# A decoder layer in fp32 on one core: the first step's weight rounding moved to pair 5, LayerNorm roots behind the second maxima, a new order of the fourth batch, identity products between the first maxima

## What is computed

```python
def reference(x, ctx_512, ...):
    x = _layernorm(x + _L0_attn_ref(x, wq, wk, wv, wo))       # 16 heads, causal, rope
    x = _layernorm(x + _L0_xattn_ref(x, ctx, Wq, Wkv_expand, Wout))
    x = _layernorm(x + _L0_ffn_ref(x, weight1, weight2, weight3))

def _L0_ffn_ref(x, weight1, weight2, weight3):
    w1, w2, w3 = nf4_roundtrip(weight1), nf4_roundtrip(weight2), nf4_roundtrip(weight3)
    h = silu(einsum('bsd,fd->bsf', x, w1)) * einsum('bsd,fd->bsf', x, w2)
    return einsum('bsf,df->bsd', h, w3)

def _layernorm(x, eps=1e-05):
    return (x - mean(x)) / sqrt(var(x) + eps)
```

## Time and profile before

| | |
|---|---|
| median of 3 runs | 1119.15 us (1118.89 to 1129.97) |
| profiled execution | 1125.64 us, span 1123.9 us |
| mean granted clock of TensorE | 0.976 |
| PE busy | 1038.3 us (92%) |
| DVE busy | 755.5 us (67%) |
| ACT busy | 482.4 us (43%) |
| POOL busy | 439.8 us (39%) |
| chain that ended last | PE 67%, DVE 19%, issue 5%, DMA 3%, POOL 3% |

### The profile page before, as it was taken

How to read it: one execution, slowest core, us unless ns; L and a number is a source line. 1 busy time by engine, 2 the same in 40 slices (tenths; PEclk the granted TensorE clock), 3 DMA queues, 4 the chain that set the end, 5 groups by cost and what they waited for, 6 DMA issues and landing times.

```text
span 1123.9 us, 17522 instructions
## 1 busy us (share of the span) xinstructions
PE 1038.3 (92%) x6280; PEld 670.4 (60%) x6280; DVE 755.5 (67%) x1560; ACT 482.4 (43%) x587; POOL 439.8 (39%) x462
## 2 busy tenths in 40 slices
PE   9899999999999898998989998998989999999995
PEld 7545455555455454565546556555636888888884
DVE  7778658666866688559676876877673546464535
ACT  3343445554464464546654664676442212112110
POOL 3448675975786564123352432334257000000000
PEclk9899999999999999999989999999989999999998
DMA  6731586386636674646755485757445202011021
GB/s 232 216 91 30 140 220 180 90 242 179 191 84 169 189 203 102 160 92 147 208 140 125 116 202 127 166 147 183 111 135 163 83 1 105 8 38 38 1 75 38
DMA packets 92618, 145.16 MB, mean 129 GB/s; under 512 B 22507, under 2 KB 39795, under 8 KB 92275
## 3 DMA queue, kind: packets, MB, share of 16 engines
q1 hardware_dynamic: 83218, 116.49, 39.8%
q0 software_dynamic: 8000, 26.75, 8.3%
q10 hardware_dynamic: 1312, 0.79, 0.2%
HBM read 78.09 MB, written 23.73 MB: 91 GB/s over the span
## 4 chain that ended last, share of the span: by engine, by line
PE 67%; DVE 19%; issue 5%; DMA 3%; POOL 3%; ACT 2%; SPq 1%; ACTq 0%; DVEq 0%; POOLq 0%
PE att_pv L1041 11%; PE att_scores L978 7%; PE att_scores L1294 7%; PE att_pv L1294 7%; PE att_scores_T L1324 7%; PE att_scores_T L962 6%; PE att_scores_T L1014 5%; PE att_scores_T L964 5%; PE att_scores_T L963 5%; DVE att_mx L1653 4%; PE att_scores_T L1159 2%; DVE att_scores L1648 2%; DVE att_nf_zone L1808 2%; DMA att_nf_home<-nf_reciprocals 2%; DVE att_stats L1684 1%
## 5 line engine op out<-in xcount | busy, mean ns | idle before, releaser
L1461 ACT ACTIVATE att_probs<-att_scores_T 128x1024 f32<-128x1024 f32 (+2 forms) x256 | 218.3, 885 | 161.7 <-PE att_scores_T L1014 159.1
L1041 PE MATMUL att_pv<-att_probs,att_v 128*32 128x512 f32 (+3 forms) x1024 | 216.6, 539 | 7.9 <-POOL att_probs L842 7.1
L1041 PE MATMUL att_pv<-att_probs,att_ones 128*32 128x512 f32 (+3 forms) x1024 | 216.6, 539 | 0.0
L1653 DVE TENSOR_REDUCE att_mx<-att_scores 128x2 f32<-128x1024 f32 x124 | 151.5, 1222 | 86.1 <-PE att_scores L978 85.3
L978 PE MATMUL att_scores<-att_k_stack,att_q_stack 96*128 96x256 f32 (+1 forms) x504 | 168.8, 407 | 32.2 <-DVE att_mx L1653 23.1
L1648 DVE CUSTOM_DVE_ANT_0 att_scores<-att_scores,att_cmask 128x128 f32<-128x128 f32 (+3 forms) x256 | 120.9, 511 | 40.6 <-PE att_scores L978 39.4
L1014 PE MATMUL att_scores_T<-att_q_stack,att_k_stack 97*128 97x512 f32 (+2 forms) x512 | 140.3, 386 | 7.7 <-ACT att_raw L1399 2.3
L978 PEld LDWEIGHTS att_scores<-att_k_stack,att_q_stack 96*128 96x128 f32 x504 | 88.3, 195 | 80.5 <-DVE att_mx L1653 32.8
L842 POOL TENSOR_SCALAR_AFFINE_SELECT att_probs<-att_probs 128x256 f32<-128x256 f32 x128 | 59.0, 461 | 164.8 <-ACT att_probs L1461 159.5
L1014 PEld LDWEIGHTS att_scores_T<-att_q_stack,att_k_stack 97*128 97x128 f32 x512 | 87.7, 195 | 49.4 <-issue 18.9
L1547 ACT ACTIVATE att_probs<-att_scores 128x512 f32<-128x512 f32 x44 | 26.3, 598 | 208.0 <-PE att_scores L1294 208.0
(11 more groups left out here) (262 smaller groups left out, 2102.3 us busy)
## 6 DMA issues: line engine op xcount, KB each, us to landing
att_q_stack<-att_q_hi SPq DMA_DIRECT2D x128, 128.0 KB, 3.2
att_probs<-nf_x SPq DMA_DIRECT2D x28, 352.0 KB, 3.5
att_nf_home<-nf_reciprocals POOLq DMA_DIRECT2D x48, 176.0 KB, 4.8
att_q_stack<-att_q_lo SPq DMA_DIRECT2D x64, 128.0 KB, 3.6
att_k_stack<-att_k_hi SPq DMA_DIRECT2D x64, 128.0 KB, 3.5
att_nf_home<-nf_x SPq DMA_DIRECT2D x20, 352.0 KB, 3.6
w_nf<-att_nf_zone SPq DMA_DIRECT2D x192, 22.0 KB, 2.5
att_k_stack<-att_k_hi SPq DMA_DIRECT2D x64, 64.0 KB, 4.1
```

Source lines behind the costliest of these rows:

```text
L1041: last = T.matmul(pv[HD * j:HD * j + HD, sums, q0:S], lhs, pr[:, at:at + S - q0], start=(t == 0), stop=(t == TT - 1))
L1461: A.activation(probs_of(b, r)[:, 1024 * h:1024 * h + w], bank[:, 0:w], ACT.Exp, scale=SCALE).then_inc(st_free, 1)
L1653: V.tensor_reduce(mx[:, p % 2, :].rearrange("p (r t) -> p r t", r=2)[:, :, t], sco[:, :, :], AX.X, ALU.max).then_inc(sc_free, 1)
```

## The change

Five edits, which leave every result the same.

1. At the start PE multiplies the identity by itself five times ahead of each of the maxima of pair 1, t = 1, 2, 3.
2. `round_steps` leaves out pair 0 of every self attention batch, and takes pair 5 instead of leaving it out. So (1, 5) and (2, 5) carry a round each, (2, 0) and (3, 0) none. The number of rounds in self attention stays 20.
3. In batches 1 and 2 the whole of `spread` stands behind the second maxima (t = 1) of pair 2; its first part stood at the end of pair 1, its second ahead of these maxima. `scale_rows` stands behind the rounding's last pass.
4. In batch 3 the third maxima (t = 2) come directly behind the second on DVE, and the fourth ahead of pass 3, as in cross attention; on PE the projections of the next batch stand between them accordingly.
5. In batch 3 `spread` stands in one piece behind the third maxima of pair 3, and `scale_rows` of pair 4 behind the third maxima and behind pass 3.

```diff
@@ -104,7 +104,7 @@
-            if b < B and p == 5 or b == B - 1 and p > 4 or (b, p) in ((1, 0), (B, 0)):
+            if b < B and p == 0 or b == B - 1 and p > 4 or (b, p) == (B, 0):
@@ -1199,6 +1199,9 @@
             for t in range(1, TT):
+
+                for i in range(5):
+                    T.matmul(bank_for(("exp", 0, 0, 0))[:, 0:P], ident[:, :], ident[:, :], start=True, stop=True)
                 maxima(0, 1, t)
@@ -1236,7 +1239,7 @@
-                    elif crossed(b) and whats:
+                    elif late(b) and whats:
@@ -1867,8 +1870,6 @@
                         moments(b - 1, 1)
-                        if not late(b):
-                            begin_spread(range(TT))
@@ -1879,11 +1880,7 @@
-                    if b > 0 and not late(b) and p == 2:
-                        end_spread(range(TT))
-                    if b == B - 1 and p == 3:
-                        begin_spread(range(TT))
-                    if (b, p) == (B - 1, 4) or (b, p) == (NB - 1, 5):
+                    if (b, p) == (NB - 1, 5):
                         scale_rows(range(0, 2), TT - 1)
@@ -1891,22 +1888,18 @@
                     if b > 0 and not late(b) and p == 2:
-                        scale_rows(range(TT), TT - 1)
+                        spread(range(TT))
-                    quick = crossed(b) and bool(made(b + 1, p))
+                    quick = late(b) and bool(made(b + 1, p))
                     if quick:
                         maxima(*fore, 2)
-                    if crossed(b) and p == 3:
-                        begin_spread(range(TT))
                     if late(b) and p == 3:
-                        end_spread(range(TT))
+                        spread(range(TT))
-                    if b == B - 1 and p == 4:
-                        scale_rows(range(2, TT), TT - 1)
-                    if quick and b > B and p == 5:
+                    if quick and (b > B and p == 5 or (b, p) == (B - 1, 4)):
                         scale_rows(range(0, 2), TT - 1)
@@ -1928,8 +1921,10 @@
                     exceeds(end, (1, 2, 3) if beside else (3,))
-                    if quick and b > B and p == 5:
+                    if quick and (b > B and p == 5 or (b, p) == (B - 1, 4)):
                         scale_rows(range(2, TT), TT - 1)
+                    if b > 0 and not late(b) and p == 2:
+                        scale_rows(range(TT), TT - 1)
```

## The result

| | before | changed |
|---|---|---|
| median | 1120.52 us (4 runs, 1118.89 to 1129.97) | 1141.98 us (4 runs, 1138.08 to 1145.53) |
| profiled execution | 1125.64 us, span 1123.9 | 1141.23 us, span 1139.5 |
| mean granted clock | 0.976 | 0.977 |
| PE busy | 1038.3 us | 1040.1 us |

The ratio is 1.0152 (95% interval 1.0112 to 1.0192): slower by 1.5%, 17 us. The forecast was +7.7 us, 1126.8 us with a range to 1133.0. The direction was right, the size was less than half of the measured one.

A forecast was written before the change was run, and what follows sets the result against it. TensorE, busy 92% of the span, was taken to bound the kernel, so shifts of each touched step's last matmul were added: +7.7 us in sum, median 1126.8 us from 1119.15, own range 1123 to 1131, wider range 1116.0 to 1133.0.

The forecast's parts named there:

- Identity products: Start, ahead of step (0,0): products may keep the clock up, but VectorE's row bounds this stretch; -0.5 us, bounds +1.1 and -2.3.
- Rounding taken from pair 0: Steps (2,0) and (3,0): the wait for pass 3 and the rounding's length go; -1.9 and -2.1 us.
- Rounding put at pair 5: Steps (1,5) and (2,5): VectorE's passes wait for GpSimd's operations; +4.3 us each, and +1.3 each for low clock.
- A wait at (1, 7): Step (1,7): TensorE's 0.59 us wait for the rounding before goes, as its load comes sooner; -0.6 us.
- Roots behind the second maxima: Step (1,2): VectorE pays the roots after idling, +0.7 us; step (2,2): TensorE's wait and low clock go, -1.1 us.
- The fourth batch: Steps (3,2) to (3,6): waits for fourth maxima go, but pass 3 comes late; +2.0 us, bounds +0.9 and +3.4.
- pair 5 is cheap: Rival: passes slip between GpSimd's operations, both +4.3 become +0.9 and the clock stays; -1.7 us, median 1117.5; chance 0.22.
- All that is new also waits: Rival: roots in (2,2) gain nothing, fourth batch costs its upper bound, one pair 5 costs 6; 11.9 us, 1131.1; chance 0.15.
- the start: Rival: clock stays full at the start, later stretch goes, freed transfers at (3,0) pay; +3.5 us, 1122.7; chance 0.10.

## Why the prediction fell short

The terms of the forecast against the step lengths of the changed kernel's profile:

*Identity products, -0.5:* measured +0.2, and no difference in time in the run with them alone. Right in its reason, and in the price: ten records took 1.04 us (34.95 to 35.99), where 1.1 was forecast.

*Rounding taken from pair 0, -1.9 and -2.1:* -1.0 over (2, 0) and (2, 1), and -5.4 over (3, 0) and (3, 1). The direct gain is 2.3 and 2.9 us here and 1.7 to 2.6 in the other runs with the edit, near the 2.1 and 2.2 worked out. In (3, 1) the 2.5 us are the low clock that lay at 389.8 in the execution before; the runs with the products alone and with the order alone lose it too (-2.3 and -3.0), with the rounding of (3, 0) in place. Not an effect of the change, so that this pair of steps did better than forecast is luck.

*Rounding put at pair 5, +4.3 each and +1.3 for the clock:* the mechanism was right, pass by pass: three DVE passes, each 0.38 us behind a GpSimd operation. Two sizes were off. The wait in (1, 5) was 4.97, not 3.6, for GpSimd's operations stood 1.4 us earlier in the step, so that the first pass met the next one, which ends 1.1 us later in the step than the one it was to meet; the forecast took the order of before as fixed in time. Wait and rounding together, 5.7 us, stayed under the +6 named as the upper bound. In (2, 5) the wait was 3.88, close to the forecast, although the operations do not stand "in the same places" there: before, L779 begins 1.6 us into (2, 5) and 4.1 us into (1, 5). They come every 2.5 us, so in both steps one of them ends 6.5 us into the step, and this is what counts. And the low clock lasted 6.8 us in both places: (1, 5) and (1, 6) grew by 7.6 us, of which wait and rounding are 5.0 + 0.7, and (2, 5) and (2, 6) by 6.9, of which they are 3.9 + 0.7; the rest, 1.9 and 2.3 us where 1.3 was taken, is put down to the clock. The upper bound of 1.7 was too low, since a stretch can be twice as long as the one it was read from; the earlier trace rows itself has one of 10.3 us. Together 15.2 us over (1, 5), (1, 6), (2, 5) to (2, 7), against 11.2.

*A wait at (1, 7), -0.6:* measured -0.6, by luck: the runs with the products alone and with the row scaling in pair 3, in which no rounding moved, have the same.

*Roots behind the second maxima, +0.7 and -1.1:* measured +1.5 and -0.7. The signs came out as forecast, the second of them with help from the clock (1.9 us of (2, 2), see the run with the roots alone). The place was wrong: the steps themselves became shorter, and the next ones longer, by the scaling of the rounding that now comes behind the four scaled rows (waits of 1.18 and 2.00 us). The prediction had called the row scaling behind the passes free, "it lies beside PE's projection". That it hides the scaling's instructions does not hide what is queued behind them on DVE.

*The fourth batch, +2.0 with a bound of +3.4:* measured +9.0 over (3, 2) to (3, 7) in the changed kernel's profile, and 11.6 us by the times of the run with it alone. This is the term that failed: it lies furthest outside its own bounds (+0.9 to +3.4), and with 7.0 us it is the largest part of what the forecast lacks. In (3, 2) the working was right: +1.5 forecast, a wait of 1.85 seen and the step 2.0 longer. In (3, 3), measured +3.9, it gave +0.3 for 3.4 us of roots and the passes, all at the lengths that they have alone, in the same prediction that priced passes at pair 5 by GpSimd's operations. The roots took 6.2 us (433.27 to 439.50) and the passes 2.35, so PE waited 4.61 us and got the low clock for 6.8 us from 441.9 on. The kernel before had these roots stretched to 7.3 us in two parts, in the very step that the forecast read. In (3, 4), measured +1.6 for +0.4, the wait for the maxima that should go (1.67) went, and 2.52 for pass 3 came. No instruction of DVE is stretched there: the two rows scaled take 1.0 us, the passes 0.6 each, and it is the number of instructions in front of pass 3 that makes the wait. (3, 6) and (3, 7) were 0.65 and 0.45 us longer, in every run that has edit 4 and in no other; the forecast had -0.2 from (3, 5) on. What the forecast did not do was to write out the row of DVE between the second maxima and pass 3 for these two steps as it did for (3, 2), with GpSimd's timeline beside it.

*The rivals:* "pair 5 is cheap" was wrong, as the waits show. "All that is new also waits" was nearest: its mechanism, DVE late behind what stands in front, is what happened, with a price for the fourth batch (+3.4) of little over a third of the real one. Nothing of the outcome came from the start. The sum was wrong for the fourth batch first (7.0 us), then for pair 5 (4.0 us) and for the roots of batches 1 and 2 (1.3 us); the lucky steps (3, 0) and (3, 1) took 3.3 us of this back.

## What to carry to other kernels

Before moving VectorE work that reads and writes SBUF, write out VectorE's whole row in front of the instruction that TensorE waits for, lay GpSimd's timeline beside it, and count for each instruction there the rest of the GpSimd operation that it meets; do it for every instruction moved, the tiny ones too, and not only for the one that caught the eye. A wait of 4 to 5 us on TensorE should be priced with the low clock behind it, here 6.8 us at half speed, about another 2 us. And a step that gets shorter is no gain until the next step's first waits have been read: work taken from between two maxima comes back in front of what is queued behind it.

## What the runs showed of the hardware

A VectorE instruction that GpSimd holds up ends when GpSimd's operations end, almost whatever its own size. In the changed kernel one on 128 x 4 numbers took 2.79 us (0.17 alone), and passes on 128 x 1408 took up to 2.7 (0.6 alone); in the run with the row scaling in pair 3 two row scalings took 5.61 us (1.0 alone). Its own size shows only in how far its end stands behind GpSimd's: 0.38 us for a pass, 0.28 for a row scaling (198.05 behind 197.77), 0.04 for the small one (436.47 behind 436.43). Reductions of maxima, which read PSUM, took 1.18 to 1.24 us in every kept profile, also with the same operations beside them (228.53 above, beside that of 228.31). The Trainium skill's page "SBUF — State Buffer" (section "SBUF: two separate sides") names which instructions take the shared ports, two SBUF inputs or a two-port mode, and that the side that came second blocks fully; the trace agrees with both: 2.79 against 0.17 us for the one kind, 1.21 us unchanged for the reductions. One thing the rows leave open: the instruction of 433.68 is recorded 0.2 us before GpSimd's of 433.88 and is blocked all the same, and by two operations, so the start in a row is not always the moment that decides which of the two is first. The instructions of 417.03 and 420.97 in the kernel before and the row scaling of 192.44 start 0.3 to 0.4 us ahead in the same way. In all four GpSimd is issuing a DMA at that moment (the row of 432.81 above) and starts its operation straight behind it. The first pass of 439.54 starts 0.3 us ahead of an operation (439.84) with no such issue and keeps its 0.59 us. Whether the issue is the reason no run here tests.

In the changed kernel the granted clock fell to 0.50 for 6.8 us towards the end of each wait of 3.9 to 5 us (from 230.3, 349.7 and 441.9); in the run with the rounding alone for 10.2 us once (from 350.2). For shorter waits there is no rule in these runs. Behind the waits of 1.85 and 2.52 us of the changed kernel it did not fall, but behind one of 2.49 us in the run with the order alone it did (6.8 us from 445.0); with ScalarE's passes it fell at the wait of 2.93 us and not at that of 2.94. It also fell in places that no edit touches, at different moments in each execution. The times of the kernel before go with it: its fastest run, 1116.4 us, has a mean granted clock of 0.984, its slowest, 1135.2 us, one of 0.974.
